# Patch tokens of the second group placed by transfers of their own, and the last patch product issued behind the second pair's scores

## The reference

```python
patches = extract_patches(x, 16)                       # (32, 16, 768)
h = einsum('bnd,dh->bnh', patches, W) + b + pos_emb    # (32, 16, 192)
h = concatenate([h, txt], axis=1)                      # (32, 48, 192)
h = h + attention(layernorm(h))    # 12 heads of 16, rope, causal, Wo
h = h + moe(layernorm(h))          # 8 experts, top 2, capacity 480
```

## Time and profile before

| | |
|---|---|
| runs | 265.55 us median, 263.51 to 265.73 |
| the profiled execution | 265.56 us, its span 263.4 us |
| TensorE busy in the span | 241.3 us (92%) |
| VectorE, ScalarE, GpSimd | 169.3, 131.0, 121.4 us |
| attention and routing | to about 132 us |
| experts | to about 255 us, then the last scatter |

### The profile page before, as it was taken

The page is one execution under the profiler, slowest core; times in us unless marked ns, Lnnn a source line. Parts: engine busy times, 40 slices in busy tenths (PEclk is TensorE's granted clock), DMA queues, the critical chain, the costliest instruction groups (busy, mean ns, idle before and its releaser), DMA issues.

```text
span 263.4 us, 5689 instructions
## 1 busy us (share of the span) xinstructions
PE 241.3 (92%) x2072; PEld 194.8 (74%) x2077; DVE 169.3 (64%) x534; ACT 131.0 (50%) x349; POOL 121.4 (46%) x135
## 2 busy tenths in 40 slices
PE   7999979999999999998999999999999999999910
PEld 2857756666776677676669989898999989898900
DVE  7374558888878887978936683747658283852300
ACT  0216665878687577865264471634527170722300
POOL 8052534432663476161660181735537180828370
PEclk9999999999999999999999999999999999999995
DMA  7990189700012101542127966675775767423140
GB/s 215 304 289 2 32 207 330 289 2 21 31 46 75 56 33 34 153 119 60 40 79 188 255 96 183 143 189 134 139 185 87 207 82 183 81 28 38 19 47 9
DMA packets 26107, 31.02 MB, mean 118 GB/s; under 512 B 3197, under 2 KB 22961, under 8 KB 25824
## 3 DMA queue, kind: packets, MB, share of 16 engines
q1 hardware_dynamic: 18560, 20.81, 29.5%
q0 software_dynamic: 6144, 8.59, 16.3%
q10 hardware_dynamic: 1376, 1.26, 1.8%
HBM read 20.34 MB, written 10.08 MB: 115 GB/s over the span
## 4 chain that ended last, share of the span: by engine, by line
PE 73%; DVE 12%; POOL 4%; DMA 3%; issue 3%; SPq 1%; ACT 1%; DVEq 0%; POOLq 0%
PE bank L734 14%; PE scores L725 5%; PE scores L726 5%; PE scores L718 5%; PE scores L722 5%; PE scores L719 5%; PE bank L420 3%; PE bank L456 3%; PE bank L434 3%; PE bank L505 3%; PE scores L484 2%; PE bank L435 2%; PE bank L703 2%; DMA early<-in_patches 2%; PE scores L477 2%
## 5 line engine op out<-in xcount | busy, mean ns | idle before, releaser
L1450 POOL DMA_INDIRECT out_rows<-blank,tok x32 | 56.6, 1769 | 61.7 <-DVE blank L1325 54.7
L946 ACT ACTIVATE blank<-scores 128x480 f32<-128x480 f32 (+1 forms) x33 | 18.4, 559 | 59.2 <-PE scores L726 59.2
L734 PE MATMUL bank<-w_sb,blank 128*120 128x192 f32 x224 | 37.7, 326 | 0.0
L734 PEld LDWEIGHTS bank<-w_sb,blank 128*120 128x120 f32 x224 | 36.2, 183 | 0.1
L1398 POOL DMA_INDIRECT slots<-rows,slot x24 | 24.4, 1016 | 22.6 <-issue 11.5
L1336 DVE TENSOR_TENSOR blank<-blank,scores 128x480 f32<-128x480 f32 (+1 forms) x33 | 21.0, 639 | 21.2 <-ACT blank L946 21.2
L1325 DVE SCALAR_TENSOR_TENSOR blank<-bank,keys,blank 120x192 f32<-120x192 f32 x32 | 11.5, 412 | 26.5 <-DMA out_rows<-blank,tok 20.9
L718 PE MATMUL scores<-z0h,wah 128*128 128x480 f32 x64 | 25.3, 396 | 0.0
L725 PE MATMUL scores<-z,wbh 128*128 128x480 f32 x64 | 24.5, 382 | 0.3 <-DVE z L1321 0.3
L726 PE MATMUL scores<-z,wbl 128*128 128x480 f32 x64 | 24.5, 383 | 0.0
L722 PE MATMUL scores<-z0l,wah 128*128 128x480 f32 x64 | 24.3, 380 | 0.0
(11 more groups left out here) (204 smaller groups left out, 527.2 us busy)
## 6 DMA issues: line engine op xcount, KB each, us to landing
early<-in_w SPq DMA_DIRECT2D x8, 512.0 KB, 4.9
early<-in_w SPq DMA_DIRECT2D x16, 256.0 KB, 6.2
w_sb<-in_w SPq DMA_DIRECT2D x8, 384.0 KB, 3.8
slots<-blank POOLq DMA_DIRECT2D x2, 1515.0 KB
keys<-slots SPq DMA_DIRECT2D x8, 378.8 KB, 5.1
early<-in_patches SPq DMA_DIRECT2D x4, 384.0 KB, 8.1
h_all<-in_hinit SPq DMA_DIRECT2D x1, 864.0 KB, 7.8
tokw_all<-in_tokw ACTq DMA_DIRECT2D x1, 576.0 KB, 4.1
```

Source lines behind the costliest of these rows:

```text
L734: mm = pe.matmul(o, hT[:, m, c * CR:(c + 1) * CR], w2_sb[:, par, m, :], start=(m == 0), stop=(m == MH - 1))
L946: act.activation(sg[:, m % 2, cols], up_bank[2 * (m % 2)][:, cols], ACT.Silu).then_inc(s_silu, 1)
L1450: pool.indirect_dma_start(out=out, out_offset=bass.IndirectOffsetOnAxis(ap=tok[:, e, c:c + 1], axis=0), in_=yw[:, c, :], in_offset=None, b ...
```

## The change

`place_patches` gets the range of groups as an argument. SP waits for two groups' tokens and places group 1 by eight transfers (16 rows of 192 in each); groups 2 and 3 follow after the fourth group's tokens in five transfers, and three on GpSimd, as before. TensorE issues the last patch product in pair 1 behind `scores(1)` and `turn_probs(0)` and ahead of `turn_qk`. VectorE takes the statistics of group 1 in pair 0, behind `patch_tokens(2)` and a wait for the eight transfers, and `patch_tokens(3)` in pair 1 behind `shift(1)`. GpSimd's `rstd` of group 1 moves to the top of pair 0. The waits for the other transfers move to pair 2.

```diff
-        def place_patches(queue, batches, done):
+        def place_patches(queue, batches, groups, done):
...
-                queue.dma_start(hg[at % P:at % P + NPATCH, 1:GROUPS, at // P, :],
-                                ptok_sb[b * NPATCH:(b + 1) * NPATCH, 1:GROUPS, :]).then_inc(done, 16)
+                queue.dma_start(hg[at % P:at % P + NPATCH, groups, at // P, :],
+                                ptok_sb[b * NPATCH:(b + 1) * NPATCH, groups, :]).then_inc(done, 16)
...
+            sp.wait_ge(s_ptok, 2)
+            sp.wait_ge(s_h, 16)
+            place_patches(sp, range(GTOK // S), slice(1, 2), s_ptok_in)
             sp.wait_ge(s_ptok, GROUPS)
-            sp.wait_ge(s_h, 16)
-            place_patches(sp, range(5), s_ptok_in)
+            place_patches(sp, range(5), slice(2, GROUPS), s_ptok_in)
...
                 scores(j)
                 if back:
                     turn_probs(j - 1)
+                if j == 1:
+                    pe.wait_ge(s_ptok, 3)
+                    patch_product(3, b6)
...
                     v_product(j)
-                if j == 0:
-                    pe.wait_ge(s_ptok, 3)
-                    patch_product(3, b6)
...
                 if j == 0:
                     patch_tokens(2, b6)
+                    dve.wait_ge(s_ptok_in, 16 * (GTOK // S))
+                    statistics(range(GT, 2 * GT), GT)
+                if j == 1:
+                    patch_tokens(3, b6)
...
-                if 1 <= j < GROUPS:
-                    if j == 1:
-                        dve.wait_ge(s_ptok_in, 16 * 5)
+                if 2 <= j < GROUPS:
+                    if j == 2:
+                        dve.wait_ge(s_ptok_in, 16 * (GTOK // S + 5))
                         dve.wait_ge(s_ptok_pool, 16 * 3)
                     statistics(range(GT * j, GT * (j + 1)), GT + j - 1)
...
-                if j == 0:
-                    patch_tokens(3, b6)
...
+                if j == 0:
+                    rstd(range(GT, 2 * GT), GT)
                 if qk is not None:
                     rotated(qk)
...
-                    place_patches(pool, range(5, GTOK // S), s_ptok_pool)
-                if 1 <= j < GROUPS:
+                    place_patches(pool, range(5, GTOK // S), slice(2, GROUPS), s_ptok_pool)
+                if 2 <= j < GROUPS:
                     rstd(range(GT * j, GT * (j + 1)), GT + j - 1)
```

## The result

The changed kernel takes **271.59 us** (median of six, 270.84 to 271.96) against 265.02 of six runs of the kernel before on the same chip: ratio 1.0254, 95% interval 1.0217 to 1.0290. It is slower by 6.6 us, outside the forecast's 263.9 to 268.3.

What follows compares the result with a forecast made beforehand. TensorE, busy 92% of the span, was taken as the bound, so only its waits count. Removing waits gave -1.2 and late expert weights +1.7, so 265.56 + 0.5 = 266.1 us, range 263.9 to 268.3.

Steps and rivals of the forecast that it cites:

- First transfers and statistics: Group 1's eight placements land at 24.2 us; statistics of tiles 3 to 5 move to pair 0 at added cost 0.
- Last patch product, what goes: TensorE: moving twelve matmuls to pair 1 costs nothing; the turn of tile 3 comes at about 36.3, gaining 1.2 us.
- The zero transfers go out 3.6 us earlier: GpSimd's two large slots<-blank transfers go out at 33.3 instead of 36.94 us, turning their order against expert 0's weights.
- What is late next, "2.3 us of cover": SP's last placement of groups 2 and 3 lands at 35.9 us, 2.3 before VectorE wants it at 38.2.
- rival 3: Zero transfers catch SP's two last placements, landing at 39.4; statistics of tiles 6 to 8 1.2 late: 265.6 us, chance 0.08.
- one packet for one: DMA queues: while the zero transfers run, SP's queue passes as many packets as theirs, 256 of 12 KB.
- The weights, L = 50.0: Expert 0's weights land at L = 50.0 us; ScalarE's split and TensorE's values(3) wait, changing the time by L - 49.5.
- rival 2: Zero transfers win wholly; expert 0's weights land at 51.8, ScalarE stops 4.2 us at its split: 267.9 us, chance 0.15.

Runs made afterwards that it cites:

- e1: The changed kernel with GpSimd waiting for SP's placements to land before it issues the two zero transfers: 262.55 us, ratio 0.9945.
- e1b: The same kernel as e1, run again beside e9 on its chip: 263.43 us, ratio 0.9951.
- e9: The changed kernel with the last patch product back at the end of pair 0 and the zero transfers behind SP's placements: 263.45 us, ratio 0.9967.
- e2: The changed kernel with 4 and 7 idle matmuls put into the two TensorE waits between 41.7 and 44.8 us: 267.07 us, ratio 1.0105.
- e5: The changed kernel with the last patch product and its token addition back at the end of pair 0: median 267.34 us, ratio 1.0058.
- e3: The kernel before with only the two zero transfers moved to right behind GpSimd's three placements in pair 0: 275.02 us, ratio 1.0401.
- e7: The changed kernel with one of the two zero transfers moved to pair 2: median 271.05 us, one run of four at 264.80.
- e10: The changed kernel with three of the last placements on SP and five on GpSimd, instead of five and three: median 269.79 us, ratio 1.0011.
- e6: The changed kernel with the two zero transfers issued ahead of GpSimd's loop over pairs: median 270.55 us, ratio 1.0168.
- e4: The kernel before with only the last patch product and its token addition moved to pair 1: 271.19 us, ratio 1.0272.
- e8: The kernel of e4 with 16 idle matmuls before the turn of tile 3: 267.00 us, ratio 1.0097.

## Why the prediction was wrong

*First transfers and statistics*: right. Group 1's placements landed at 25.6 (24.2 forecast) and the rotation of tile 2 began at 27.51 instead of 26.48, but as argued this cost nothing: the turn of tile 2 came at 30.46.

*Last patch product, what goes*: right. scores(2) stayed (33.77), the turn of tile 3 came at 36.03 (36.3 forecast), and 1.4 to 1.5 us were won there. e1, e1b and e9 show what is left of it at the end, near the forecast's 1.2: 1.4, 0.6 and 0.6 us by their medians, 1.5, 1.3 and 0.9 by their ratios.

*The zero transfers go out 3.6 us earlier*: right, 33.18 against 33.3 forecast. On this step, together with the later placements, everything turned.

*What is late next, "2.3 us of cover"*: **this step failed.** It took the landing from the earlier trace rows, where nothing else moved, and priced the zeros only for the weights behind them. Measured was a landing at 40.91 in place of 35.9, and in place of 2.3 us of cover a wait of VectorE of 2.96. The same turn of order stood in the text as rival 3, with a chance of 0.08 and a delay of 3.5 us; measured were 5.1 (7.24 - 2.1), and rival 3's chain is what happened. The reasoning "one packet for one" gave the placement too little delay. The Trainium skill, "DMA: Bandwidth & Descriptors" (Queues, rings and completion order), says that each engine goes round between the queues it has work for, packet by packet. The counts of the microsecond from 39 (36 against 31) agree; those from 36 to 39 (33 against 1 in the lowest) do not, unless SP's queue had nothing ready then, which the trace does not show.

*Rival 3's price, "the gain is gone at once: 265.6"*: too low, and mostly by a **missing term**. By that price TensorE would have been level with the kernel before; it was 1.4 us later at the turn of tile 3's k, since the landing came 1.5 later than rival 3's 39.4. And no step priced a standing TensorE in clock: its fall added 5.4 to the stretch up to values(3) (3.9 of the whole by e2). Nothing in the kernel before showed a fall there, with a wait of 1.13 us; that a longer one would bring it was not asked.

*The weights, L = 50.0*: 1.9 too early, and just above rival 2's 51.8. The last piece was issued at 38.5, not at the 36.9 of 35.5 + 1.35: SP's issues took longer than before (the blank rows 1.44 us in place of 0.59). It landed 13.4 later, at 51.9:

```profile
L372 SPq DMA_DIRECT2D early<-in_w x2: 1351/1382/1412, 37.1 to 38.5; - x2
...
DMA to landing us min/median/max: 11.8/12.0/13.4
```

But the stop before it hid it: the split came at 53.62 without waiting. In e2, where the clock's part was taken away, and in e5, where the earlier stop was, ScalarE's wait (1.51 and 2.62 us) and TensorE's at values(3) (0.75 and 1.84) appear as the prediction described them, and in e5 near its L (49.6).

## What to carry to other kernels

When a step is taken off a queue, ask what was standing behind it: here a wait on GpSimd had kept two large transfers away from small urgent ones, and in the kernel before only that wait had done so (e3). Price a new TensorE wait twice, once for its length and once for the clock behind it; a few idle matmuls in the wait separate the two. And order small urgent transfers against large ones by a wait on their landing (e1, e9). Putting half as much in front did not help in three runs of four (e7), and keeping them clear of one large transfer left them to another (e10).

## What the runs showed of the hardware

- A small placement issued some 0.5 us (e6: 1.6) behind the first large transfer of the other queue took 7 to 9 us to land instead of 2: 7.2 (changed kernel), 9.2 (e3), 7.9 (e6, e7), 7.1 (e10, with the queues the other way round). With the zeros held back it took 3.6 (e1) and 2.9 (e9) at the most. In e5, issued half a microsecond ahead of the zeros, it was not caught. Why SP's queue passes almost nothing for a while is not settled.
- TensorE's granted clock fell to 0.50 in or after single waits of 8.30 us (e3), 5.87 (e6), 3.72 (e4) and 1.84 (e5, the profiled execution), and after 0.92 and 1.58 us with little work between (changed kernel; much the same in e7 and e10); it stayed at 1.00 with 1.13 us (kernel before) and where the waits were filled (e2, e8). In the changed kernel the low level lasted for about 13 us, although TensorE was busy all the while from 45 on. The Trainium skill, "TensorE: Matmul & The Clock Gate" (Part 1: The HAM clock gate), says that the clock follows how busy the engine has lately been. On the fall the rows agree, and e2 and e8 show it. Why the low level lasts so long under a busy engine no run here settles.
- One program can have a wide spread of times: e5, e7 and e10 ran from 262.5 to 272.5 us. The shortest time of each went with its highest mean granted clock (0.981 to 0.984, the others 0.955 to 0.981). How much of such a spread is lateness and how much clock is not shown, since only one execution of each was profiled.
